# Tridiagonalisation of a 64 x 64 matrix: a new order for VectorE's norm, update of S, scalars and u.y

## What is computed

```python
def _L0_gnn_ref(features, A, W1, b1, W2, b2):
    deg = jnp.sum(A, axis=0) + jnp.sum(A, axis=1) - jnp.diagonal(A)
    d_inv_sqrt = jnp.where(deg > 0, jax.lax.rsqrt(deg), 0.0)
    L = jnp.diag(deg) - A
    L_norm = d_inv_sqrt[:, None] * L * d_inv_sqrt[None, :]
    _, U = jnp.linalg.eigh(L_norm)
    agg = jnp.einsum('mn,bnd->bmd', U.T, features)
    h = jax.nn.relu(agg @ W1 + b1)
    out = h @ W2 + b2
    return jnp.einsum('nm,bmd->bnd', U, out)
```

## Time and profile before

| | |
|---|---|
| median of three runs | 2159.38 us |
| the profiled execution | 2159.02 us |
| its span in the trace | 2157.2 us (1.8 us lie around it) |
| tridiagonalisation | from 19.0 to about 213.5 us of the span |
| split, sweeps and joins | to about 486 us |
| the features' layers | to the end |

### The profile page before, as it was taken

One profiled execution on the slowest core, in us unless ns is written; L12 is line 12 of the kernel. 1 busy time (PEld: TensorE's weight loads), 2 busy tenths in 40 slices (PEclk: granted clock), 3 DMA queues, 4 the chain that ended last, 5 costly groups with the idle time before them and its releaser, 6 DMA issues. The chain is left out here.

```text
span 2157.2 us, 32357 instructions
## 1 busy us (share of the span) xinstructions
PE 1800.1 (83%) x9764; PEld 1546.3 (72%) x9764; DVE 1440.8 (67%) x5776; ACT 857.7 (40%) x1768; POOL 658.5 (31%) x1044
## 2 busy tenths in 40 slices
PE   3454334325999999999999999999999998989997
PEld 2333333314999788888899999988887886868885
DVE  7999999985778465454444444534445677868885
ACT  2333222201434466233333333323332555656664
POOL 0001344412233367433233333423332112531121
PEclk9999766656999999999999999999999999989999
DMA  6000000000111000000000000000010411210111
GB/s 191 2 2 1 1 1 1 1 1 20 60 40 50 20 15 20 10 10 5 10 11 10 10 0 10 20 1 0 0 39 10 158 67 52 98 59 21 50 40 50
DMA packets 44689, 62.72 MB, mean 29 GB/s; under 512 B 13968, under 2 KB 33296, under 8 KB 44432
## 3 DMA queue, kind: packets, MB, share of 16 engines
q1 hardware_dynamic: 43968, 61.08, 8.4%
q10 hardware_dynamic: 592, 0.17, 0.0%
HBM read 36.08 MB, written 25.17 MB: 28 GB/s over the span
## 5 line engine op out<-in xcount | busy, mean ns | idle before, releaser
L2273 ACT ACTIVATE l_gates<-ps,biases 128x512 f32<-128x512 f32 (+1 forms) x504 | 288.8, 635 | 490.6 <-remote 476.1
L2144 PE MATMUL ps<-l_nodes_in,l_even 128*128 128x512 f32 x1392 | 321.3, 391 | 2.6 <-DVE x L1562 1.9
L2144 PEld LDWEIGHTS ps<-l_nodes_in,l_even 128*128 128x128 f32 x1392 | 260.9, 188 | 59.0 <-DVE x L1562 2.7
L2144 PE MATMUL ps<-l_nodes_in,kept 128*128 128x336 f32 (+1 forms) x1280 | 298.0, 350 | 1.9 <-ACT l_gates L2273 1.8
L2370 DVE TENSOR_TENSOR l_gates<-l_gates 128x512 f32<-128x512 f32 (+1 forms) x72 | 50.2, 697 | 343.2 <-ACT l_gates L2273 343.2
L2060 POOL CAST l_nodes_in<-big 128x512 fp32r (+3 forms) x142 | 100.3, 735 | 549.7 <-remote 520.0
L2144 PEld LDWEIGHTS ps<-l_nodes_in,kept 128*128 128x128 f32 x1280 | 229.4, 188 | 27.3 <-issue 4.3
L2144 PE MATMUL ps<-l_state,l_even 128*128 128x512 f32 x960 | 223.3, 392 | 0.0
L2144 PEld LDWEIGHTS ps<-l_state,l_even 128*128 128x128 f32 x960 | 180.4, 188 | 39.6
L2063 POOL TENSOR_TENSOR l_nodes_in<-big,l_nodes_in 128x512 fp32r<-128x512 f32 (+1 forms) x142 | 200.4, 1433 | 5.7
L995 PE MATMUL ps<-w,sw_xT 128*128 128x128 f32 x256 | 59.7, 427 | 126.3 <-ACT sw_xT L859 126.3
(11 more groups left out here) (567 smaller groups left out, 3906.9 us busy)
## 6 DMA issues: line engine op xcount, KB each, us to landing
x<-in_x SPq DMA_DIRECT2D x4, 2048.0 KB, 16.9
residual<-s_x SPq DMA_DIRECT2D x16, 512.0 KB, 2.6
x<-residual SPq DMA_DIRECT2D x16, 512.0 KB, 9.1
normed<-l_raw SPq DMA_DIRECT2D x16, 512.0 KB, 2.6
x<-normed SPq DMA_DIRECT2D x16, 512.0 KB, 3.2
out<-a_y SPq DMA_DIRECT2D x16, 512.0 KB, 2.8
l_raw<-in_L_gnn_W SPq DMA_DIRECT2D x16, 256.0 KB, 2.7
l_raw<-in_L_gnn_W SPq DMA_DIRECT2D x4, 512.0 KB, 3.8
```

The source lines that it names most:

```text
L2144: return pe.matmul(ps[:, 4 * j + gate, 0:n], weight[w_part][:, at:at + 128].bitcast(F32R), src[:, part, k, 0:n].bitcast(F32R), start=start ...
L2273: act.activation(gates[:, j, gate, 0:n], ps[:, 4 * j + gate, 0:n], ACT.Tanh if gate == G else ACT.Sigmoid, bias=bias[:, gate * KD + j:gate ...
```

## The change

Four things are moved on VectorE within a step; no instruction is added or taken away, and the other engines' programs stay as they are.

- `norm2` stands right behind `row` and `b_pu`, ahead of `minus_update` and `b_p`.
- `x` and `update` stand further back: `x` behind `signed`, `update` behind `m`, which was the first instruction of `scalars` and now has a function of its own.
- `betas` stands in front of `uy`, and `b_y`, which was in `betas`, behind `uy`.
- `minus_update` stays ahead of `r_col`, `b_p` is behind it.

```diff
@@ -235,13 +235,15 @@
-            def scalars(i):
-
-
-                head = rows[i % 2][:, i + 1:i + 2]
+            def m(i):
                 after(("signed2", i), ("inv", i), ("signed", i))
                 stt(col("m", i), col("signed2", i), col("inv", i), col("signed", i), ALU.mult,
                     ALU.add).then_inc(m_ready, 1)
+
+            def scalars(i):
+
+
+                head = rows[i % 2][:, i + 1:i + 2]
                 dve.wait_ge(m_ready, i + 1)
                 dve.wait_ge(r_col_ready, i + 1)
                 tt(head, col("m", i), head, ALU.add).then_inc(chain[0], mark("head", i))
@@ -253,22 +255,23 @@
                 stt(col("b", i), col("tail2", i), 0.0, col("inv_m", i), ALU.is_gt,
                     ALU.mult).then_inc(chain[0], mark("b", i))
 
+            def betas(i):
+                after(("b", i), ("inv_head", i))
+                tt(col("beta", i), col("b", i), col("inv_head", i), ALU.mult).then_inc(chain[0], mark("beta", i))
+                after(("beta", i))
+                tt(col("b_beta", i), col("b", i), col("beta", i), ALU.mult).then_inc(chain[0], mark("b_beta", i))
+                dve.wait_ge(u_ready, i + 1)
+                tt(col("b_u", i), col("u_col", i), col("beta", i), ALU.mult).then_inc(b_u_ready, 1)
+
             def uy(i):
                 r, e = rows[i % 2], i + 1
                 dve.wait_ge(y_ready, i + 1)
                 ttr(junk[2][:, e:], y[i % 2][:, e:], r[:, e:], 1.0, 0.0, ALU.mult, ALU.add,
                     col("uy", i)).then_inc(chain[0], mark("uy", i))
 
-            def betas(i):
+            def b_times_y(i):
                 e = i + 1
-                after(("b", i), ("inv_head", i))
-                tt(col("beta", i), col("b", i), col("inv_head", i), ALU.mult).then_inc(chain[0], mark("beta", i))
-                if e < STEPS:
-                    ts(b_y[:, e + 1:], y[i % 2][:, e + 1:], col("b", i), None, ALU.mult).then_inc(chain[0], mark("b_y", i))
-                after(("beta", i))
-                tt(col("b_beta", i), col("b", i), col("beta", i), ALU.mult).then_inc(chain[0], mark("b_beta", i))
-                dve.wait_ge(u_ready, i + 1)
-                tt(col("b_u", i), col("u_col", i), col("beta", i), ALU.mult).then_inc(b_u_ready, 1)
+                ts(b_y[:, e + 1:], y[i % 2][:, e + 1:], col("b", i), None, ALU.mult).then_inc(chain[0], mark("b_y", i))
 
@@ -288,20 +291,24 @@
                 if i:
                     row(i)
                     b_pu(i - 1)
-                    minus_update(i - 1)
-                    b_p(i - 1)
                 norm2(i)
                 if i:
-                    x(i - 1)
+                    minus_update(i - 1)
                 r_col(i)
                 if i:
-                    update(i - 1)
+                    b_p(i - 1)
                 signed2(i)
                 signed(i)
+                if i:
+                    x(i - 1)
+                m(i)
+                if i:
+                    update(i - 1)
                 scalars(i)
+                betas(i)
                 uy(i)
-                betas(i)
                 if i + 1 < STEPS:
+                    b_times_y(i)
                     mix(i)
```

## The result

The changed kernel takes 2165.18 us (median of 9 runs, 2164.72 to 2167.1) against 2159.63 us for the kernel before on the same chips (9 runs, 2158.45 to 2161.17): a ratio of 1.0027, 95% interval 1.0017 to 1.0037, so **5.6 us or 0.27% slower**. The forecast was 2168.5 us, in a range from 2157 to 2174, with a chance of 0.70 for slower by more than 0.2%.

A forecast was written before the change was run, and what follows sets the result against it. VectorE's chain bounds the tridiagonalisation, busy 186.8 of 194.5 us. Per step -0.22 (row to m), +0.09 (m to head) and +0.28 (head to row) give +0.15, 9.2 us in all: 2168.5 us, range 2157 to 2174.

The forecast's parts named there:

- Row to m: Middle step, from row's start to m's start: m at 1.13 to 1.18 us, 0.2 earlier than before.
- m to head: Middle step: m held until 1.50, update starts at 1.43, head at 1.60 us, 0.13 before the old 1.73.
- the likeliest case: m stays held by GpSimd's subtraction in all or most steps; slower by over 0.2%, chance 0.70.
- the first rival: m escapes the hold, update ends about 0.04 later, head at 1.43 to 1.47: 2158 to 2161 us; chance 0.14.
- the 0 to 0.05 allowed for the wait in front of minus_update: Extra us in row to m, as minus_update waits for two semaphores behind an instruction that was itself waiting.
- Head to the next row: Middle step, chain through b, beta, b_beta, b_y, mixed: 1.60 us against 1.32 before, 0.28 more.
- (c): VectorE instructions with several semaphores to wait for may cost more issue time: b 0.15 behind inv_head, mixed 0.21 behind b_beta.
- The sum: Whole step: -0.22, +0.09 and +0.28 make +0.15 us a step, 9.2 us more over 61 steps.
- What costs nothing: uy does not wait for y, TensorE's own and p add no wait at pu, GpSimd and DMA cost nothing.
- the 6 us kept for it at the upper end: Two thirds of a possible wait of pu for p, 0.14 a step or 8.5 us in all.
- That the order makes no difference: Rival: each VectorE instruction starts only when the last left the pipe, so time stays 2159.4 us; chance 0.07.
- The faster case: Rival: m and update run free and b's gap closes, -0.10 us a step, 2153 us; chance 0.09.

The follow-up runs named there:

- late_wait_kept: Changed kernel with VectorE's own late wait written first before b and mixed, so the instruction itself carries it: 2156.0 us, ratio 0.9981 to before.
- front_alone: Changed kernel with the old order from b on (uy, beta, b_y, b_beta), so only the first half of the change: 2161.7 us, ratio 1.0006 to before.
- tail_alone: Kernel before with only beta, b_beta and b_u moved ahead of uy and b_y, old order up to head: 2181.0 us, ratio 1.0099.
- all_three: Changed kernel with late waits carried by the instruction, GpSimd's subtraction also waiting for own, and b_y ahead of uy: 2146.5 us, ratio 0.9934 to before.
- b_y_first: Changed kernel with b_y ahead of uy, both behind b_u: 2160.2 us, ratio 0.9999 to before.

## Why the prediction was right, and where its steps were not

*Row to m: right.* m was forecast at 1.13 to 1.18 and came at 1.12, and GpSimd 0.80 behind half_sign, as forecast: the separate wait in front of minus_update costs nothing, as it clears long before it is reached.

*m to head: the likeliest case was wrong, the first rival's was right.* I took m as held, with head at 1.60; it ran free, and the update was held instead. The sign named for the forecast, m still 0.33 long, did not come. It hung on the 0 to 0.05 allowed for the wait in front of minus_update: that was 0, and m came 0.07 ahead of GpSimd. The rival had the update end 0.04 late; it was 0.07, and head at 1.48, beyond its 1.47 and well short of 1.60. How near the edge lay, two steps of the changed kernel show. In an early one m starts 0.03 ahead of GpSimd and is free, in a later one, by the rounded rows, it is 0.03 ahead too and held (unrounded, 0.037 and 0.025):

```profile
31.20 0.20 DVE L240 SCALAR_TENSOR_TENSOR td_c_m<-td_c_signed,td_c_inv 64x1 f32<-64x1 f32 x1
31.23 0.35 POOL L398 TENSOR_TENSOR eg_qT<-eg_qT,td_turned 64x64 f32<-64x64 f32 x1 [3.04 <-ACT td_turned L341]
31.33 0.34 DVE L235 SCALAR_TENSOR_TENSOR sym<-td_row,td_c_x,td_minus_S 64x61 f32<-64x61 f32 x1
```

```profile
180.75 0.35 DVE L240 SCALAR_TENSOR_TENSOR td_c_m<-td_c_signed,td_c_inv 64x1 f32<-64x1 f32 x1
180.78 0.31 POOL L398 TENSOR_TENSOR eg_qT<-eg_qT,td_turned 64x64 f32<-64x64 f32 x1 [2.83 <-ACT td_turned L341]
181.03 0.22 DVE L235 SCALAR_TENSOR_TENSOR sym<-td_row,td_c_x,td_minus_S 64x15 f32<-64x15 f32 x1
```

Most steps are on the free side: 0.03 to 0.07 ahead in the first half, 0.07 to 0.11 in the second. In the early step GpSimd, with the update beside it, takes 0.35 itself instead of 0.31.

*Head to the next row: right in kind, too small by 0.09.* The two bare hand-offs, 0.19 and 0.18, were read correctly from head to inv_head. The term "mixed waits for b_y's end, 0.24 + 0.04" should have been 0.37. The rows had it: the same two instructions, 0.37 apart. I charged it under (c) as issue time behind b_beta, as if it would vanish in a real wait, when it stands behind one. late_wait_kept shows what it is.

*The sum: right in part by luck.* The two misses, -0.12 at the head and +0.09 in the tail, nearly cancelled: 3.17 instead of 3.20. With head at 1.48 and the tail as forecast, the step would have been 3.08, 0.03 above before, or 2 us, which a measurement does not tell from no change; with head at 1.60 and the tail as measured, 3.29 and 15 us. So that the change is clearly slower was owed to a wait that the forecast had too small.

The mean over the stage is +0.10 a step where +0.15 was forecast for all: 5.6 us measured, 9.2 forecast. In the middle step it is +0.12, so 0.03 of the difference is the sum's. The loss does depend on the row's length, against my "The waits hardly depend on the row's length": the first step went from 3.26 to 3.41, one of the last from 2.89 to 2.97. But the long rows lose more than the middle one and the short ones less, so over the stage this nearly averages out. The rest, 0.02 a step or 1 us, lies in single steps in which VectorE stands still for longer in one kernel than in the other: in the kernel before, the row with 40 elements starts at 93.34 and the next at 96.75, 3.41 later, with 0.23 of idle in front of minus_update that no result ended, where its neighbour took 3.11 and the same step of the changed kernel 3.23. What stops VectorE there is open.

*What costs nothing: right.* uy did not wait for y, pu did not wait for p (p starts at 125.01 and takes 0.42, pu starts at 125.90), so the 6 us kept for it at the upper end were not needed. front_alone shows the wait for y that moving uy avoids.

*Rivals.* That the order makes no difference is out: orders of the same instructions lie 19 us apart (tail_alone and front_alone). The section of the Trainium skill that the prediction names for it (VectorE: DVE Perf Modes, The DRAIN you can't avoid) adds that an operation that is not held starts earlier, so the page does not forecast this rival as plainly as the prediction has it. The trace agrees with that addition: 0.07 from beta to b_y. The faster case asked for b's gap to close with the update in front of head; the gap stayed at 0.15 and only closed when the wait was rewritten.

## What to carry to other kernels

In a chain of short dependent instructions, a filler is worth what it covers: count for each pair of neighbours the bare hand-off (end plus 0.04 here) and move independent work into it; moving work out of such gaps cost 0.35 us a step (tail_alone), more than the 0.25 that the other half won up to the head. Write the wait that will clear last so that the instruction itself carries it, and look in the trace at who stands beside GpSimd: in this kernel those two things were worth 16 us, and the new order of VectorE had only moved the first onto the update and left the second in place.

## What the runs showed of the hardware

- GpSimd's subtraction with two inputs in SBUF holds a VectorE instruction with two inputs in SBUF: m takes 0.34 instead of 0.21 and ends 0.32 behind GpSimd's start, the update takes 0.31 instead of 0.24 and ends 0.37 behind it. A clearing of one column by GpSimd at the same moment holds nothing, and mixed, with one input in SBUF and one in PSUM, is not held by the subtraction (all_three).
- The edge is narrow. For m it lies at about 0.03 us ahead of GpSimd's start: held at 0.030 (late_wait_kept, 172.82), free at 0.033 (the change, first step). It is not the same for every instruction: `signed` was free 0.02 ahead (the change, 192.95), and `x` was held 0.04 ahead (b_y_first, 34.15, 0.37 long).
- A semaphore wait in an instruction of its own costs nothing when it is over early (minus_update, two semaphores, 0.06 behind half_sign) and 0.07 to 0.10 when it clears late.
